# A new order of VectorE and TensorE in the attention stage of a one-core Macaron block (8 x 1024 tokens, width 256)

## What is computed

```python
x = x + 0.5 * moe(layernorm(x))        # 8 experts, top 2, capacity 1024 each
x = x + attn(layernorm(x))
x = x + 0.5 * moe(layernorm(x))

def attn(x):                           # B=8, T=1024, C=256, 16 heads of 16
    q, k, v = split(x @ w_qkv.T); q, k = rope_xpos(q, k)
    scores = (q @ k.T) / 4 * decay_mask            # causal, gamma_h ** (t - s)
    y = scores @ v
    yn = groupnorm(y over (16 channels, T) of each head) * gn_weight + gn_bias
    return (silu(x @ w_gated.T) * yn) @ w_proj.T

def moe(x):                            # scores = softmax(x @ router_w)
    for k in range(2):                 # first choice, second choice
        slots = first 1024 tokens of each expert, in order of token
        out += scatter(gelu(x[slots] @ w1[e]) @ w2[e]) * weight_k
```

## Time and profile before

| | |
|---|---|
| runs | 2335.0 us median of 3 (2325.99 to 2337.48) |
| profiled execution | 2339.04 us, span 2337.2 us |
| busy share of the span | PE 93%, DVE 58%, POOL 50%, ACT 42% |
| mean granted TensorE clock | 0.965 of full speed |
| attention | from about 911 to about 1490 us of the span, the drain to about 1560 |

### The profile page before, as it was taken

One profiled execution on the slowest core, in us unless ns is written; L12 is line 12 of the kernel. 1 busy time (PEld: TensorE's weight loads), 2 busy tenths in 40 slices (PEclk: granted clock), 3 DMA queues, 4 the chain that ended last, 5 costly groups with the idle time before them and its releaser, 6 DMA issues.

```text
span 2337.2 us, 57530 instructions
## 1 busy us (share of the span) xinstructions
PE 2165.9 (93%) x22289; PEld 1907.2 (82%) x22289; DVE 1362.6 (58%) x3363; ACT 987.9 (42%) x2173; POOL 1163.2 (50%) x911
## 2 busy tenths in 40 slices
PE   7869999999999997998899889839999999999998
PEld 6759999999999986776777677638899999999997
DVE  7755555555555543578777777655455555555553
ACT  4434444444444432455545554433344444444442
POOL 5755777644444433223333443365777745454443
PEclk9999999999999998999999989859999999999999
DMA  9523444444434424101212120234444444444432
GB/s 365 204 80 68 105 86 106 91 96 89 97 88 97 88 51 131 40 21 58 76 40 59 59 76 22 60 95 125 104 84 100 93 102 90 95 90 95 90 79 32
DMA packets 169414, 212.01 MB, mean 91 GB/s; under 512 B 50732, under 2 KB 147568, under 8 KB 165104
## 3 DMA queue, kind: packets, MB, share of 16 engines
q1 hardware_dynamic: 111888, 140.24, 18.0%
q0 software_dynamic: 57344, 69.21, 17.6%
HBM read 138.39 MB, written 73.14 MB: 91 GB/s over the span
## 4 chain that ended last, share of the span: by engine, by line
PE 50%; DVE 6%; issue 3%; ACT 1%; POOL 0%; another core or an unknown queue 0%; POOLq 0%; DMA 0%; DVEq 0%; ACTq 0%
PE bank L695 16%; PE bank L677 15%; PE bank L797 10%; PE bank L885 2%; PE bank L918 1%; PE bank L868 1%; PE bank L664 1%; PE bank L853 1%; PE bank L903 1%; PE bank L815 1%; DVE aw L1798 1%; DVE dl L1505 0%; DVE gsm L1854 0%; DVE rt L1786 0%
## 5 line engine op out<-in xcount | busy, mean ns | idle before, releaser
L1132 ACT ACTIVATE h<-bank 128x512 f32<-128x512 f32 x512 | 306.0, 598 | 853.8 <-PE bank L677 719.6
L1702 DVE CAST hh<-h 128x512 fp32r<-128x512 f32 x512 | 239.9, 468 | 695.9 <-ACT h L1132 582.5
L695 PE MATMUL bank<-w2h,hh 128*128 128x256 f32 x2048 | 579.2, 283 | 3.1 <-ACT yb L1150 3.1
L695 PE MATMUL bank<-w2l,hh 128*128 128x256 f32 x2048 | 573.8, 280 | 0.0
L695 PE MATMUL bank<-w2h,hl 128*128 128x256 f32 x2048 | 573.7, 280 | 0.0
L695 PEld LDWEIGHTS bank<-w2h,hh 128*128 128x128 f32 x2048 | 385.1, 188 | 45.5 <-ACT yb L1150 3.6
L695 PEld LDWEIGHTS bank<-w2h,hl 128*128 128x128 f32 x2048 | 384.8, 188 | 41.6
L695 PEld LDWEIGHTS bank<-w2l,hh 128*128 128x128 f32 x2048 | 385.2, 188 | 39.7 <-issue 0.3
L677 PE MATMUL bank<-xh,w1h 128*128 128x512 f32 x1024 | 405.2, 396 | 5.8 <-issue 5.1
L677 PE MATMUL bank<-xh,w1l 128*128 128x512 f32 x1024 | 404.5, 395 | 0.0
L677 PE MATMUL bank<-xl,w1h 128*128 128x512 f32 x1024 | 404.1, 395 | 0.0
(11 more groups left out here) (218 smaller groups left out, 3299.2 us busy)
## 6 DMA issues: line engine op xcount, KB each, us to landing
stg<-in_L_ffn_w SPq DMA_DIRECT2D x64, 1024.0 KB
xb<-acc SPq DMA_DIRECT2D x9, 1024.0 KB, 5.5
xa<-in_L_attn_x SPq DMA_DIRECT2D x8, 1024.0 KB, 14.2
xn_rows<-xa SPq DMA_DIRECT2D x8, 1024.0 KB
xn_rows<-xn_r SPq DMA_DIRECT2D x8, 1024.0 KB
xr<-acc SPq DMA_DIRECT2D x7, 1024.0 KB
out_rows<-xr SPq DMA_DIRECT2D x7, 1024.0 KB
slot_table<-pay,idx POOLq DMA_INDIRECT x256
```

The lines of the kernel that those rows point to most:

```text
L695: product = pe.matmul(tile_sum(j, t, end), a[:, fj, t * P:(t + 1) * P], c[:, fj, :], start=(fj == 0 and i == 0 and (end or t % 2 == 0)), s ...
L1132: act.activation(h32[fj % 2][:], bank[fj % 2][:], ACT.Gelu_apprx_tanh).then_inc(f.gelu, 1)
L1702: dve.tensor_copy(hh[:, fj, :], h32[fj % 2][:]).then_inc(f.hh, 1)
```

## The change

Three edits of order and one of an instruction.

1. **PE.** `head_means` goes behind `attend(n)` and `scores(n + 1, 0)`, `head_variances` behind `scores(n + 1, 1)`, `counts` from before `attend(n + 2)` to before `attend(n + 4)`. `BANK_FILLS` follows.
2. **DVE.** The statistics of the next layer norm leave the first half of a batch: `front_stats(b + 2, ...)` now stands at the end of `sequence(b)`, one pair before `residual_shift` and three pairs behind the last `carry`. `residual_choices(b - 1)` stands there too, instead of at the start of the next batch. `channels` goes behind `mask(n, 1)`, `head_variance` and `affine` later, and `choice_part`, `places` and `slot_entries` are spread over the second half.
3. Several masks and rotations swap places on DVE.
4. `exponent_scale` clamps with a `scalar_tensor_tensor` (the greater of the value and -87, then the lesser of that and 1) instead of a `tensor_scalar`. Its values are never above 0.

```diff
 # PE sequence(b)
                 new_state(n + 1, 0)
-                head_means(b - 1)
                 attend(n)
                 scores(n + 1, 0)
+                head_means(b - 1)
                 new_state(n + 1, 1)
-                head_variances(b - 1)
...
                 scores(n + 1, 1)
+                head_variances(b - 1)
...
-                counts(b - 2)
                 attend(n + 2)
...
                 new_state(n + 5, 1)
+                counts(b - 2)
                 attend(n + 4)
 # exponent_scale(b)
-                dve.tensor_scalar(dls[:], dls[:], -87.0, None, ALU.max).then_inc(S.scaled, 1)
+                floor = ones[:, 0:NT * E].rearrange("p (t e) -> p t e", e=E)
+                dve.scalar_tensor_tensor(dls[:], dls[:], -87.0, floor, ALU.max, ALU.min).then_inc(S.scaled, 1)
 # DVE sequence(b), the new text of its first part
                 mask(n, 0)
                 channel_stats(n - 1)
                 rotate(n + 2)
                 mask(n, 1)
                 channels(b - 1)
                 carry(n + 1, 0)
                 mask(n + 1, 0)
                 about_head(b - 1)
                 carry(n + 1, 1)
                 rotate(n + 3)
                 mask(n + 1, 1)
                 carry(n + 2, 0)
                 head_variance(b - 1)
                 rotate(n + 4)
                 mask(n + 2, 0)
                 carry(n + 2, 1)
                 channel_stats(n)
                 affine(b - 1)
                 mask(n + 2, 1)
                 exponent_scale(b - 2)
                 choice_part(b - 2, 0)
                 gating(b - 1, 0)
                 carry(n + 3, 0)
                 rotate(n + 5)
                 gating(b - 1, 1)
                 mask(n + 3, 0)
                 gated_low(b - 1, 0)
                 carry(n + 3, 1)
                 gated_low(b - 1, 1)
                 mask(n + 3, 1)
...
 # and its end
                 residual_variance(b - 1)
                 rotate(n + 9)
+                residual_choices(b - 1)
                 front_low(b + 1, 3)
+                front_stats(b + 2, 0)
                 channel_stats(n + 6)
                 residual_shift(b - 1)
                 carry(n + 8, 1)
+                for j in range(1, NT // 2):
+                    front_stats(b + 2, j)
```

More of the change, by code:

```diff
@@ L1947, in sequence @@
                 channel_stats(n - 1)
-                residual_choices(b - 2)
-                front_stats(b + 1, 0)
+                rotate(n + 2)
+                mask(n, 1)
                 channels(b - 1)
-                mask(n, 1)
-                rotate(n + 2)
                 carry(n + 1, 0)
+                mask(n + 1, 0)
                 about_head(b - 1)
-                front_stats(b + 1, 1)
-                head_variance(b - 1)
-                mask(n + 1, 0)
                 carry(n + 1, 1)
-                front_stats(b + 1, 2)
                 rotate(n + 3)
@@ L1962, in sequence @@
                 carry(n + 2, 0)
+                head_variance(b - 1)
+                rotate(n + 4)
+                mask(n + 2, 0)
+                carry(n + 2, 1)
                 channel_stats(n)
                 affine(b - 1)
-                front_stats(b + 1, 3)
+                mask(n + 2, 1)
                 exponent_scale(b - 2)
-                mask(n + 2, 0)
                 choice_part(b - 2, 0)
-                choice_part(b - 2, 1)
-                places(b - 2, 0)
                 gating(b - 1, 0)
-                mask(n + 2, 1)
-                carry(n + 2, 1)
-                places(b - 2, 1)
-                rotate(n + 4)
+                carry(n + 3, 0)
+                rotate(n + 5)
                 gating(b - 1, 1)
-                carry(n + 3, 0)
+                mask(n + 3, 0)
                 gated_low(b - 1, 0)
-                mask(n + 3, 0)
+                carry(n + 3, 1)
                 gated_low(b - 1, 1)
-                rotate(n + 5)
-                carry(n + 3, 1)
                 mask(n + 3, 1)
                 front_variance(b + 1)
+                choice_part(b - 2, 1)
                 residual(b - 1, 0)
                 mask(n + 4, 0)
-                places(b - 2, 2)
                 carry(n + 4, 0)
+                places(b - 2, 0)
                 mask(n + 4, 1)
@@ L1993, in sequence @@
                 carry(n + 4, 1)
-                places(b - 2, 3)
-                places(b - 2, 4)
+                residual_stats(b - 1, 0)
+                residual_stats(b - 1, 1)
                 carry(n + 5, 0)
                 rotate(n + 7)
-                residual(b - 1, 2)
-                slot_entries(1, b - 2)
-                residual_stats(b - 1, 0)
                 front_low(b + 1, 0)
                 carry(n + 5, 1)
+                places(b - 2, 1)
+                residual(b - 1, 2)
                 mask(n + 5, 0)
                 residual(b - 1, 3)
-                residual_stats(b - 1, 1)
                 residual_stats(b - 1, 2)
+                residual_stats(b - 1, 3)
+                mask(n + 5, 1)
                 channel_stats(n + 1)
                 channel_stats(n + 2)
-                mask(n + 5, 1)
+                places(b - 2, 2)
                 residual(b - 1, 4)
-                residual_stats(b - 1, 3)
                 channel_stats(n + 3)
@@ L2014, in sequence @@
                 front_low(b + 1, 1)
-                residual_stats(b - 1, 4)
+                places(b - 2, 3)
                 carry(n + 6, 0)
@@ L2023, in sequence @@
                 residual(b - 1, 6)
-                residual_stats(b - 1, 6)
+                places(b - 2, 4)
+                slot_entries(1, b - 2)
                 front_low(b + 1, 2)
@@ L2039, in sequence @@
                 carry(n + 8, 1)
+                for j in range(1, NT // 2):
+                    front_stats(b + 2, j)
             def drain():
                 a, z = B - 2, B - 1
-                residual_choices(a)
                 choice_part(a, 0)
@@ L2093, in _ @@
             start_residual()
+            for j in range(NT // 2):
+                front_stats(0, j)
             for b in range(-1, B):
```

14 lines of the change are left out of this document (8 added, 6 removed).

## The result

The changed kernel takes 2363.9 us (median of 4; 2362.3 to 2370.9), beside 2334.3 us of the kernel before on the same chip: a ratio of 1.0138, 95% interval 1.0104 to 1.0172. The profiled execution took 2364.9 us with a span of 2363.1. The forecast was 2358 us and slower, which holds.

The account below looks back on a forecast made before the run. PE sets the pace, losing 10.7 us a batch to waits and clock; new waits replace them (65.7 to 76.4 us). Batches 0 and 1 add 10, clock falls 13: 2362 us, 2358 against the median; range 2328 to 2384.

Parts of the forecast that it names:

- Start of a batch: Statistics ahead of mask(n,0): PE waits 2.1 us before scores(n,1), 0.3 before attend(n); +1.6 us a batch over batch 1.
- A: Third tile: rotate(n+4) now stands before mask(n+2,0), so PE waits before scores(n+2,1); +1.2 us a batch.
- C: Fourth tile: rotate(n+5) and the second gating stand before mask(n+3,0), so PE waits for that mask; +1.2 us a batch.
- D: Fourth tile: later second gating frees bank 1 late for values(n+4), then bank 2 for queries(n+4); +2.0 us a batch.
- B: Third tile: affine behind mask(n+2,0), a carry and channel_stats delays output(n+1), so PE waits before memory(n+2); +1.7 us a batch.
- Fifth tile: Logits land late for residual(b-1,0), ahead of mask(n+4,0); DVE waits, and PE with it; +1.8 us a batch.
- `counts`: At its new place: 0.5 us of work plus 0.7 us waiting for bank 1, held by gate(b,2); +1.2 us a batch.
- Falls of the clock: Short falls in the fourth tile of batches 1 to 7, 6 us; long ones at two of seven starts, 7 us; +13.
- The second: Rival: DVE arrives late anyway, so A to D and the fifth tile fall to little; 2288 us, faster; chance 0.15.
- The first: Rival: the clock stays up, without falls in the new places; 2345 us, within 0.5%; chance 0.22.
- The third: Rival: a long clock fall in every batch from the wait before scores(n,1); 2376 to 2382 us; chance 0.2.
- The fourth: Rival: mask(n,0) comes later, not ahead; with the statistics hidden, 1.2 us less a batch, 2350 us; no separate chance.

Follow-up runs that it names:

- a4: Changed kernel with the eight statistics of the next norm moved from the batch's end into DVE's idle gaps; 1.0139 of the kernel before.
- a1: Changed kernel with mask(n+2,0), carry(n+2,1), channel_stats(n) and affine put back ahead of rotate(n+4) on DVE; 1.0126 of the kernel before.
- a2: Changed kernel with the second gating and mask(n+3,0) put back ahead of rotate(n+5) on DVE; 1.0200 of the kernel before.
- a5: Changed kernel with the edits of a1, a2 and a4 together; 1.0078 of the kernel before.
- b1: Changed kernel with head_variances back behind project(n+3), head_variance behind rotate(n+3) and affine behind carry(n+2,0), ahead of rotate(n+4); 1.0161 of the kernel before.

## Why the prediction was right, and where it was not

*Bound and view.* That PE sets the pace and loses by waits and clock holds, and the work at full clock of 377 to 387 us in every kernel is the best support for it. One reading of the earlier trace rows was wrong: the 2.2 us of waits in the slice from 1212 on are those before `attend(n)` (1.22) and before `head_means` (1.30, of which 1.0 falls in the slice); the 0.95 before `scores(n, 1)` lies ahead of it. The prediction did not count the one before `head_means`, which five of the six intervals of the kernel before have, 6.3 us in all. And the slice at 0.50 with PE busy for all 4 us, which it took as agreement with its view of the clock, shows by itself only that the clock stayed low; the release shows in the next, 1224 to 1228, where PE is busy for 3.93 us at 1.00.

*Start of a batch, 2.1 us.* Measured 1.49, with no gap between the six statistics and the mask; `attend(n)` 0.15. In a4, without the statistics, 0.84 stays, so they are 0.65 us of it. The term was +1.6 and came to about 1.64 - 1.45 = +0.2: the prediction set some 0.8 us of batch 1 against it, but the interval of 65.7 us ends with 0.99 us before `head_means`, so that with the 0.46 at `head_variances` it holds 1.45. Its row of 1.36 us `<-remote` I took as idle time to be filled, and DVE did fill it.

*A, 1.2.* Measured 1.22; a1 took it away by that order alone. *C, 1.2.* Measured 1.25, and gone in a2 and a5. *D, 2.0.* Measured 1.33; no wait for `queries` shows behind it. `gating` took 1.21 to 1.23 us all fourteen times in the changed kernel, so it paid nothing to POOL, as the prediction had it.

*B, 1.7.* Measured 1.81, and for the reason given: `affine` ended 2.9 us after the rotation had started (1239.00 to 1241.93), where 2.8 had been added up. What the step did not see is the next bound behind it. Without the rotation the `carry` ahead of `affine` waits 1.81 us in a1, so that undoing the order gave back 0.8 us of the 3.0 of A and B.

*Fifth tile, 1.8.* Wrong. DVE waited for the logits in three batches, 0.5, 0.6 and (the last one) 1.7 us, and PE waited 0.38 us for a mask in that tile of batch 4. I had what precedes the residual 2.5 us earlier in the batch, and forgot that DVE waits for PE in A to D too; this last is argued, not tested.

*`counts`, 0.7 of wait.* Measured 1.01.

*Sum before the clock.* The forecast had 76.4 us a batch. The last four intervals average 82.6; less (1 - clock) x length, 9.3, they are 73.3. The terms measured, 0.2 + 1.2 + 1.8 + 1.25 + 1.3 + 0.4 + 1.5, give 65.7 + 7.7 = 73.4. The sum was 3 us a batch too high: 1.4 in the fifth tile, 1.4 at the start, 0.7 in D, less 0.4 that `counts` and B were too low.

*Falls of the clock, +13 in all.* Undersized in the steady state: 13 us over seven batches is 1.9 each, and the last four intervals lose 9.3 each. The step named the start and the fourth tile, and was right there. It missed the third tile of batches 3 and 5, and `counts` in batches 4 and 6: 1.01 us of waiting, then ten microseconds at half clock. It also assumed that a wait has a fixed price in clock; batches 2 and 4, with the same waits at their start and 1.00 against 0.66, show that it has not.

*The total.* That 2358 us came out near 2364 is partly luck. For the six intervals the forecast makes 65.7 + 6.5 + 5 x 76.4 + at most 13 = 467 us, and they took 477.3: some 17 us less than forecast in waits and work, 27 more in clock. These 10 us, and 3 that batch 0 took beyond its 3.4, were made up by the 10.2 us that the execution got shorter behind the seventh `head_means`, mostly by a better clock in batch 7 and the drain, where the forecast had no gain. Intervals of 76 to 80 us were forecast; one of 74.3 and four of 81 to 84 were measured.

*Between the first two `head_means`, 72 to 74 us.* Measured 72.5. PE is idle for 7.7 us there (72.50 - 64.85), 5 us more than before, where 6.5 had been added up; the difference is the start of the batch again.

*Rivals.* The second needed a wait under 0.3 us at A; it was 1.22. The first fell with the clock. The third had a long fall at the start of every batch; batches 1, 4 and 5 have one there (7, 7 and 4 us) and the other four none, so the forecast's two in seven was nearer. The falls that it lacked sit elsewhere. The fourth needed the statistics hidden; a4 puts them at 0.65 us of a wait.

## What to carry to other kernels

Between two engines that hand work back and forth in a fixed order, a wait is the first visible part of a chain: before pricing its removal, follow that chain to the next place where the waiting engine meets it, and look for the bound that comes up once the first is gone. Here a1, a2, a4, a5 and b1 each shortened or removed the waits they aimed at, and the time moved by between +0.6 and -0.6%. Split a stretch into waits, clock and work before explaining it, and judge an order by several batches and executions, because the same waits cost the clock in one and not in the next. An instruction that waits in a queue (`rotate(n + 4)` or `carry` ahead of `affine`) should have nothing behind it that another engine needs sooner.
